# The close of an engine block, and the flag of unequal neighbours, in a transformer layer with routed experts

## The reference

```
x = x + attention(layernorm(x))     # linear attention: cumulative sum of phi(k) * v, 16 heads of 16
h = layernorm(x)                    # 2048 tokens of 256
logits = h @ router_w               # 8 experts
top 2 of them, softmax over the two -> scores
routed[t]  = sum over its two experts of score * (silu(g) * u) @ w2[e],   g, u = split(h[t] @ w1[e])
shared     = (silu(h @ w_gate) * (h @ w_up)) @ w_down
out        = x + routed + shared
```

## Time and profile before

| | |
|---|---|
| median of 3 runs | 362.18 us (361.78 to 362.81) |
| the profiled execution | 362.81 us |
| its span, first to last instruction | 361.2 us |
| outside the span | 1.6 us |
| TensorE busy | 342.9 us (95%) |
| GpSimd busy | 198.3 us (55%) |
| mean granted TensorE clock | 0.997 of full speed |

### The profile page before, as it was taken

The page is one execution under the profiler, slowest core; times in us unless marked ns, Lnnn a source line. Parts: engine busy times, 40 slices in busy tenths (PEclk is TensorE's granted clock), DMA queues, the critical chain, the costliest instruction groups (busy, mean ns, idle before and its releaser), DMA issues.

```text
span 361.2 us, 9304 instructions
## 1 busy us (share of the span) xinstructions
PE 342.9 (95%) x3007; PEld 259.6 (72%) x3007; DVE 236.0 (65%) x579; ACT 215.2 (60%) x389; POOL 198.3 (55%) x294
## 2 busy tenths in 40 slices
PE   7998889889999999999999999999999999999993
PEld 7877778678888888888888555556556566666662
DVE  4979984977889888787798655454544544433431
ACT  3669547878797796974545445544554555455452
POOL 4858578678474886828233842453344344444335
PEclk9999999999999999999999999999999999999998
DMA  7976171256466565554877455978486686856550
GB/s 189 385 202 162 74 138 47 86 119 187 91 181 191 119 184 111 135 163 149 238 233 182 104 67 94 102 69 114 68 115 93 89 102 79 118 91 103 87 72 10
DMA packets 77468, 46.43 MB, mean 129 GB/s; under 512 B 61040, under 2 KB 72560, under 8 KB 77040
## 3 DMA queue, kind: packets, MB, share of 16 engines
q1 hardware_dynamic: 63088, 35.08, 39.6%
q0 software_dynamic: 9664, 10.71, 19.6%
q10 hardware_dynamic: 4672, 0.07, 1.1%
HBM read 19.09 MB, written 12.97 MB: 89 GB/s over the span
## 4 chain that ended last, share of the span: by engine, by line
PE 71%; POOL 11%; DVE 7%; issue 6%; ACT 3%; DMA 1%; POOLq 0%; DVEq 0%; ACTq 0%
PE bU L1047 13%; PE bG L1047 12%; PE bD L936 7%; PE bV L1070 7%; PE bU L238 7%; PE bG L238 6%; PE bQ L1070 6%; PE bV L238 3%; POOL x_rows L571 3%; PE bK L238 3%; PE bK L1027 2%; PE bT L936 1%; PE bT L837 1%; DVE ab L1498 1%; PE bQ L238 1%
## 5 line engine op out<-in xcount | busy, mean ns | idle before, releaser
L1498 DVE SCALAR_TENSOR_TENSOR ab<-bU,sg 128x512 f32<-128x512 f32 x64 | 44.1, 690 | 69.5 <-PE bU L1047 47.5
L765 POOL DMA_INDIRECT out_y<-xs,dst_row x32 | 49.7, 1552 | 61.8 <-DMA out_y<-xs,dst_row 30.1
L1182 ACT ACTIVATE sg<-bG 128x512 f32<-128x512 f32 x64 | 38.0, 593 | 46.0 <-PE bG L1047 26.5
L571 POOL DMA_INDIRECT x_rows<-rows,slot_u x32 | 42.3, 1321 | 18.9 <-issue 9.8
L1047 PE MATMUL bG<-we,work 128*128 (+1 forms) x216 | 52.6, 380 | 0.0
L1047 PE MATMUL bU<-we,work 128*128 (+1 forms) x216 | 52.6, 379 | 0.0
L1325 ACT ACTIVATE ws_h<-ab 128x512 f16<-128x512 f32 x36 | 22.7, 630 | 41.4 <-DVE ab L1498 37.6
L1778 DVE TENSOR_TENSOR ws_h<-ab,ws_h 128x512 f16<-128x512 f32 x36 | 24.9, 693 | 20.8 <-ACT ws_h L1325 17.9
L1189 ACT ACTIVATE ah<-ab 128x512 f16<-128x512 f32 x32 | 20.1, 630 | 29.6 <-DVE ab L1498 25.6
L1047 PEld LDWEIGHTS bG<-we,work 128*128 128x128 f16 (+1 forms) x216 | 20.7, 99 | 19.5 <-issue 1.9
L1047 PEld LDWEIGHTS bU<-we,work 128*128 128x128 f16 (+1 forms) x216 | 19.8, 99 | 17.4
(11 more groups left out here) (330 smaller groups left out, 829.6 us busy)
## 6 DMA issues: line engine op xcount, KB each, us to landing
stage<-in_w_expert SPq DMA_DIRECT2D x24, 512.0 KB, 4.0
we<-in_w_shared SPq DMA_DIRECT2D x3, 1024.0 KB, 12.0
xs<-bo POOLq DMA_DIRECT2D x8, 256.0 KB, 4.4
out_y<-xs SPq DMA_DIRECT2D x8, 256.0 KB, 2.7
xs<-in_x SPq DMA_DIRECT2D x1, 1280.0 KB, 18.8
x_rows<-we SPq DMA_DIRECT2D x9, 134.0 KB
xs<-in_x SPq DMA_DIRECT2D x3, 256.0 KB, 3.6
work<-x_rows SPq DMA_TRANSPOSE x40
```

The source lines that it names most:

```text
L571: pool.indirect_dma_start(xrows, bass.IndirectOffsetOnAxis(ap=slot_u[q][:, k, t:t + 1], axis=0), rows2[q][:, t, :].bitcast(U16), None).the ...
L765: pool.indirect_dma_start(out_rows, bass.IndirectOffsetOnAxis(ap=dst_row[:, b:b + 1], axis=0), ya[b % NY], None, bounds_check=NT * P - 1, ...
L1182: act.activation(sg[q][:], src[:], ACT.Silu, scale=1.0 / WS).then_inc(S["sg_done"], 1)
L1498: dve.scalar_tensor_tensor(out=ab[q][:], in0=src[:], scalar=1.0 / WS, in1=sg[q][:], op0=ALU.mult, op1=ALU.mult).then_inc(S["a_done"], 1)
```

## The change

Two edits. The block is opened without the option, so the closing barrier also has a DRAIN on GpSimd. And the two instructions that turn a difference of experts into 16 or 0 become one: before, "equal to 0, times -16" and then "plus 16"; after, "greater than 0, times 16". The two forms differ where a difference is negative: there the first gives 16 and the second 0.

```diff
-        block = ctx.enter_context(nc.Block(no_gpsimd_drain=True))
+        block = ctx.enter_context(nc.Block())
@@
             then(pool.tensor_tensor(pad_f[:, 1:NBLK], bexp_c[:, 1:NBLK], bexp_c[:, 0:NBLK - 1], ALU.subtract))
-            then(pool.tensor_scalar(pad_f[:, 1:NBLK], pad_f[:, 1:NBLK], 0.0, -16.0, ALU.is_equal, ALU.mult))
-            then(pool.tensor_scalar(pad_f[:, 1:NBLK], pad_f[:, 1:NBLK], 16.0, None, ALU.add))
+            then(pool.tensor_scalar(pad_f[:, 1:NBLK], pad_f[:, 1:NBLK], 0.0, 16.0, ALU.is_gt, ALU.mult))
             pool.wait_ge(S["spread_in"], 2)
```

## The result

The changed kernel takes 367.13 us (median of 4 runs, 366.63 to 367.36) against 362.40 us for the kernel before in the same session: the ratio is 1.013, 95% interval 1.011 to 1.015. That is 4.7 us slower. I had forecast slower, by 1.8 us, and a range up to 367.0, which the median misses by 0.13 us.

What follows compares the result with a forecast made beforehand. TensorE bounds the kernel (95% busy, 71% of the chain), but at the end only GpSimd's last scatter and SyncE's wait remain. DRAIN +1.8 us and edit two 0, on the 362.18 us median, give 364.0 us; range 361.7 to 367.0.

Steps and rivals of the forecast that it cites:

- The end of the chain and the room there: At the kernel's end, SyncE waits for the last scatter; a GpSimd DRAIN has 0.4 us free after the landing.
- The price of the DRAIN: At the closing barrier, GpSimd's DRAIN ends 2.2 us after the last scatter lands, costing +1.8 us.
- the trip: At the close, GpSimd asks the DMA side and gets an answer; the shortest full trip was taken as 2.2 us.
- The bound that I set: At the closing barrier, the DRAIN takes at most 5.2 us after the landing, one of the longest trips: +4.8 us.
- The rows behind 2.2 and 5.2: Profile rows read as scatter landing times: 2.2 us at the least, 3.6 in the median, 5.2 at most.
- Rows 6: Profile rows cited for GpSimd's 9664 packets and for landing times of 2.2 to 5.2 us.
- The argument from the opening DRAIN: At the opening barrier, GpSimd's DRAIN takes 0.17 us, about 0.05 beyond its last memset: the price's lower bound.
- from ScalarE's: At the closing barrier, ScalarE's DRAIN takes 0.51 us beside a 0.47 us activation: a drain costs nearly nothing once idle.
- The rule of the Trainium skill: A drain waits for a fully idle engine; with a second rule, the closing DRAIN ends at about 359.5 us, cost 0.
- The second rival, the long drain: At the close, the drain looks through queues or descriptors successively, ending 10.4 us after landing: +10.0 us, 372 us; chance 0.06.
- Edit two: In the middle, one GpSimd instruction fewer saves 0.45 us, which falls into its wait for VectorE, 4.12 to 4.57: gain 0.
- Scatter 6: At the only negative expert step, it starts 1.92 us after block 5's second half, already early, so the edit costs 0.

Runs made afterwards that it cites:

- the drains alone: Separate kernel with only GpSimd drains and DMAs, nothing of the reference computed: a drain took 712 ns after eight landed DMAs, 3311 ns after forty.
- the flag alone: Kernel before with only the two instructions for 16 or 0 made one, no closing DRAIN on GpSimd: 362.13 us, ratio 0.9994.

## Why the prediction was wrong

Point by point, by its steps:

- **The end of the chain and the room there: right.** The DRAIN's end decides as soon as it passes SyncE's signal, 0.4 us after the landing. With a drain that ended 0.2 us after the landing the cost was 0 (1.0003), with one that ended 5.0 us after it, 5.0 - 0.4 = 4.6 of the 4.7 us. TensorE's last products end at 355.96 us in the profile before and at 355.42 in the one after, earlier by the same 0.5 us as the last scatter, so nothing of the 4.7 us lies before the end.
- **The price of the DRAIN: wrong, the step that failed.** I put it at 2.2 us after the landing, as one question to the DMA side and its answer. It is no trip and does not run from the landing: it is 0.082 us for each DMA that GpSimd has issued since the last drain, landed or not, one after the other, from the end of its last work on. The closing one's 6.2 us are the price of 75 (of 86, and where the 11 went stays open), and 1.2 of them lay beside the flight of the last scatter. That the forecast had the right sign owes nothing to the trip that it was worked out from. The bound that I set, 5.2 us after the landing, just held the 5.0, by accident: it came from the longest landing on `out_y`. The range ended at that bound with nothing for how the median of the kernel before itself moves (362.18 us by three executions, 362.40 with a fourth), and the result fell 0.13 us outside.
- **The rows behind 2.2 and 5.2: misread.** I took them for landings of scatters. Rows 6 give them for every DMA on `out_y`, and the rows of SyncE's stores and of the half-block scatters in the kernel before, one after the other, part them:

```profile
L379 SPq DMA_DIRECT2D out_y<-xs x8: 394/398/573, 67.9 to 203.4; - x8
...
DMA to landing us min/median/max: 2.2/2.7/5.2
...
L760 POOL DMA_INDIRECT out_y<-xs,half_dst x8: 1541/1542/1625, 235.5 to 304.5; - x8
...
DMA to landing us min/median/max: 3.7/3.7/3.8
```

  Both 2.2 and 5.2 are of SyncE's eight stores. For scatters the profile has 3.7 to 3.8 us (the eight half-block ones) and 2.7 us (the last one, by SyncE's wait). With 3.8 in place of 5.2 the upper bound would have been 3.4 us, too low for the measured 4.7.
- **The argument from the opening DRAIN: right, from ScalarE's: wrong.** GpSimd's opening DRAIN comes before its first DMA, so its 0.17 us could not show the price; the drains alone repeat it with 34 to 51 ns and none on the bill. But I put ScalarE's closing DRAIN beside it as that of an engine "without DMAs behind" it, and ScalarE had issued 36, SyncE 154 ahead of its 7 ns. These rows could have told me that DMAs behind an engine don't in themselves make its DRAIN long; the 82 ns are shown for GpSimd alone.
- **The rule of the Trainium skill** ("PSUM — Partial Sum Buffer", "Engine vs sequencer instructions": a drain waits for the engine to go fully idle) would, as the prediction read it, have given cost 0. The runs show an idle GpSimd, with all DMAs landed, taking 6.16 us over a drain. Waiting for idleness is what the drain does besides; the price is another thing.
- **The second rival, the long drain: nearest to the mechanism.** It named a length that follows "from the number of queues or descriptors it looks through one after the other", and I gave it 0.06. There is a count, but of DMAs: 40 of 16 rows cost as much as 40 of 128. Its 372 us were far too high. What I held against it, that little can be open as each scatter's predecessor but one is known to have landed, was the mistake: landed DMAs cost the same as open ones. No row of the kernel before gives the 82 ns of one DMA.
- **Edit two: right.** The 0.45 us fell into GpSimd's wait, 4.12 to 4.66 us (I had 4.57), and the flag alone has 0.9994 with 1 in its interval. Scatter 6 starts 1.84 us after the second half of block 5 (239.65 and 241.49), before 1.92: the changed value for the negative difference moved nothing that shows. (The shortest landing of a half block is 3.7 us and not 2.2, which leaves the argument more room.)

## What to carry to other kernels

Before an instruction is added at the end of a program, ask what it has to catch up on, not only what it has to wait for: a drain on GpSimd is a bill over all its DMAs since the last one. Where such a drain can't be left out, put others where GpSimd has time to spare, so that the last one has few DMAs behind it (each of them also waits for what is in flight); a wait for the landing in front of it doesn't help and puts the bill after the landing. And where a trace shows an operation only in a state that it will not be in, the range has to be worked out from each way in which its price could scale.

## What the runs showed of the hardware

- A DRAIN on GpSimd takes 34 to 51 ns plus about 82 ns per DMA that GpSimd issued since the last drain: 712 ns for 8, 3311 for 40, 4949 for 60, 7071 for 86; 7065 for 86 indirect ones; 3308 for 40 small ones. In the changed kernel 86 cost 6159 to 6166 ns, the price of 75, and why stays open.
- The closing DRAINs of SyncE (154 DMAs issued) and ScalarE (36) show no such price: 7 ns, and 0.04 us beyond the last activation.
- A DRAIN on GpSimd also waits for DMAs in flight: with four on the bill it ended 0.2 us after the landing. The count is worked off meanwhile: 6.17 us after the last descriptors with a scatter in flight, 6.16 us with all landed.
- GpSimd can, as far as one run shows, settle DMAs while issuing: a stall of 3.18 us after 113, and a drain behind the next seven of 609 ns. Its condition stays open.
